# An LN, conv-gain and FFN block for 32,768 pixels on one core: group 4's last addition goes from an accumulating DMA to VectorE, and the rows of all engines are put in another order

## The chip, the cores and the metric

One of the eight cores of a Trainium2 chip. The metric is the device time of one execution in microseconds (us). The kernel is in Bass: each engine's instructions are written out in order, and engines meet only at semaphores.

## The reference

```python
def sobel_complexity(x): ...      # edge magnitude of the channel mean, per image
def adaptive_steps(m): ...        # a step of 1 to 5 for each pixel
def _forward(x):                  # "conv"
    V = v0 + v1 + v2 + v3         # how many of four walks visit a pixel
    return x * (V / (V + 1e-06))[:, None]

x = x + _forward(_ln_c(x))                         # x is (8, 24, 64, 64)
t = _to_tokens(x)                                  # 32768 tokens of 24 channels
y = q_acc(q_acc(q_mul(_ln_t(t)) @ q_mul(W1).T) + q_mul(b1))   # q_mul: 5 exponent, 2 mantissa bits
h = relu(y)                                                   # q_acc: 5 and 10 bits, 96 hidden
t = t + q_acc(q_acc(q_mul(h) @ q_mul(W2).T) + q_mul(b2))
```

After a layernorm over channels the channel mean is zero up to rounding, so the map of edges is flat and the walks take the same steps everywhere. The kernel has a flat pass with a constant share of visits, a flag that says if a channel mean was not zero, and a second pass behind a branch that runs only if it was. Here it does not run.

## The kernel before, in words

The pixels are in eight **groups** 0 to 7; a group is a tile of 128 partitions x 24 channels x 32 pixels in float32 (384 KB). The four statistics **units** are group 0, group 1, groups 2 and 3, and groups 4 to 7. For each group the work is this, with the helper's name and line:

- SP loads the pixels (L340). TensorE sums channels and squares (L579, L589, L607), ScalarE squares the centred pixels (`square`, L425).
- VectorE centres (`centre`, L806), sums the squares of a unit (`take_var`, L813), and works out the gain of a unit in three small instructions (`conv_gain`, L832 to L837). ScalarE takes roots (`first_std` L432, `second_std` L438), VectorE inverts them (`inverse_std` L820, `second_inverse` L849) and makes the second norm (`second_norm` L854).
- `conv` is result = centred x gain: on GpSimd (L372) for groups 0, 1, 2, 4, 5 and 6, on VectorE (L844) for 3 and 7. A wait on a count of VectorE's work ahead of `conv` on GpSimd sets its place.
- `quantise` (VectorE, L863) makes the fp8 input, TensorE turns it (`turn`, L625), ScalarE copies it (`copy_turned`, L447).
- The hidden layer has three parts: `first_layer` (TensorE, L640), `round_hidden` (ScalarE, L456), `bias_relu` (VectorE, L875) and `quantise_hidden` (VectorE, L884, in a piece of two parts and a piece of one).
- `second_layer` (TensorE, L662), `round_ffn` (ScalarE, L466), `second_bias` (VectorE, L892) give `ffn_out` in float16.
- The result is conv + pixels + ffn_out. The pixels are added by an accumulating DMA from GpSimd (`add_pixels`, L360). ffn_out is added by a second one (`add_ffn_by_dma`, L366) for groups 0 to 4, and by VectorE (`add_ffn`, L903) for 5 to 7. The semaphore residual[n] counts 16 for each landed DMA.
- SP stores the result (`store`, L327) in the order written out; the second half of group 7 is stored from ScalarE (`store_last`, L473).
- `unevenness` (VectorE, four instructions, L909 to L912), `find_peak` (TensorE, L616) and `flag` (VectorE, L919 and L920) make the flag. At its end each engine loads the flag (TENSOR_LOAD, L290) and takes a branch over the second pass (L769 TensorE, L1180 VectorE, L345 SP). `keep_busy` (L675) are TensorE matmuls whose result nobody reads.

The order on every engine is a list written out by hand in the functions `first_groups`. ScalarE reads four buffers of hidden rows; everything else has two.

## Time and profile before

| what | us |
|---|---|
| median of 3 runs | 67.58 |
| lowest and highest | 67.13 and 67.95 |
| the profiled execution's own time | 67.71 |
| its span, first to last instruction | 65.8 |
| VectorE busy | 54.9 (83%) |
| TensorE busy | 52.0 (79%) |
| ScalarE busy | 44.1 (67%) |
| GpSimd busy | 23.9 (36%) |

All times inside the execution are counted from the span's start. The 1.9 us between the span and the execution's own time lie outside it. VectorE is DVE in the rows, ScalarE ACT, GpSimd POOL, TensorE PE (its weight loads PEld), and a q behind a name is that engine's sequencer. Successive instructions of one engine overlap a little, so an instruction can take 0.48 us and the next one start 0.40 us behind its start.

### The profile page before, as it was taken

Reading aid. Unit: us, or ns where it says so; the run is one execution under the profiler, and the core shown is the slowest. Engines: PE = TensorE matmul, PEld = TensorE weight load, DVE = VectorE, ACT = ScalarE, POOL = GpSimd, SP = SyncE. Lnnn points to the kernel's source line nnn. Section 1 sums busy time; section 2 is a strip of 40 time slices with the busy share of each in tenths; the row PEclk is TensorE's granted clock in tenths of the full one; section 3 lists DMA queues with packets and bytes.
Section 4 is the critical chain, followed back from the end, with each engine's and each line's share of the span. In section 5 each row is a group of like instructions: output and inputs, shape, how many; then the busy total and the mean of one; then the engine's idle time right before and its main releaser. Section 6 shows DMA issues by size and latency. Waiting matters only on the chain.

```text
span 65.8 us, 1346 instructions
## 1 busy us (share of the span) xinstructions
PE 52.0 (79%) x471; PEld 36.5 (55%) x475; DVE 54.9 (83%) x113; ACT 44.1 (67%) x67; POOL 23.9 (36%) x25
## 2 busy tenths in 40 slices
PE   2999999999999999959759978979996988460000
PEld 0334999999998999826128335518262627150000
DVE  2059957899799999799999999999999999999300
ACT  5304352287749999279999999999999994450000
POOL 2000001964830000389387989962350580000000
PEclk9999999999999999999999999999999999999655
DMA  0999999009339000001995996999999399999651
GB/s 0 240 420 350 407 405 393 17 10 181 58 60 179 0 0 0 0 0 33 198 187 103 202 228 132 187 312 233 263 286 218 73 304 291 274 284 342 251 177 36
DMA packets 4475, 12.07 MB, mean 183 GB/s; under 512 B 496, under 2 KB 752, under 8 KB 4464
## 3 DMA queue, kind: packets, MB, share of 16 engines
q0 software_dynamic: 1872, 5.11, 39.1%
q1 hardware_dynamic: 2448, 6.62, 27.0%
q10 hardware_dynamic: 144, 0.20, 0.9%
q8 instruction: 6, 0.10, 0.8%
q14 instruction: 5, 0.04, 0.2%
HBM read 3.67 MB, written 3.15 MB: 104 GB/s over the span
## 4 chain that ended last, share of the span: by engine, by line
PE 49%; DVE 16%; ACT 13%; issue 12%; DVEq 2%; ACTq 0%
PE ps_ffn L607 12%; ACT hidden_rounded L456 10%; PE ps_ffn L589 8%; PE ps_ffn L764 8%; PE ps_hidden L640 6%; DVE hidden_q L884 5%; PE ps_ffn L662 5%; PE ps_ffn L579 4%; PE ps_hidden L607 4%; DVE ffn_out L892 3%; DVE hidden_act L875 2%; ACT packed_t L447 2%; DVE result L903 2%; DVE packed L863 1%; PE ps_turned L625 1%
## 5 line engine op out<-in xcount | busy, mean ns | idle before, releaser
L456 ACT ACTIVATE hidden_rounded<-ps_hidden 128x1024 f16<-128x1024 f32 x24 | 23.8, 1031 | 0.0
L372 POOL TENSOR_TENSOR result<-centred,gain 128x768 f32<-128x768 f32 x6 | 11.2, 1866 | 21.4 <-DVE scaled_var L837 10.4
L640 PE MATMUL ps_hidden<-packed_t,w1q 96*128 96x512 fp8e5 x48 | 14.0, 380 | 1.5 <-ACT packed_t L447 0.8
L875 DVE TENSOR_SCALAR hidden_act<-hidden_rounded,b1q 128x1024 f16<-128x1024 f16 x24 | 11.5, 478 | 0.0
L425 ACT ACTIVATE squares<-centred 128x768 f32<-128x768 f32 (+1 forms) x9 | 6.8, 769 | 4.6 <-DVE centred L806 4.6
L662 PEld LDWEIGHTS ps_ffn<-w2q,hidden_q 128*128 128x128 fp8e5 x168 | 7.6, 98 | 2.9 <-DVE hidden_q L884 2.4
L360 POOL DMA_DIRECT2D result<-loaded x8 | 8.4, 1103 | 1.8 <-POOL result L372 1.5
L662 PE MATMUL ps_ffn<-w2q,hidden_q 128*128 128x96 fp8e5 x168 | 8.3, 206 | 0.7 <-DVE hidden_q L884 0.7
L884 DVE TENSOR_SCALAR hidden_q<-hidden_act 128x2048 uint16<-128x2048 uint16 (+1 forms) x16 | 8.8, 549 | 0.1
L607 PEld LDWEIGHTS ps_ffn<-squares,loaded 128*128 128x128 f32 x72 | 8.6, 192 | 0.4
L607 PE MATMUL ps_ffn<-squares,loaded 128*128 128x128 f32 x72 | 8.7, 275 | 0.0
L806 DVE SCALAR_TENSOR_TENSOR centred<-ps_values,loaded 128x768 f32<-128x768 f32 (+1 forms) x9 | 7.5, 863 | 0.1
L863 DVE TENSOR_TENSOR packed<-centred,ps_values 128x768 fp8e5<-128x768 f32 x8 | 7.4, 946 | 0.0
L366 POOL DMA_DIRECT2D result<-ffn_out x5 | 4.6, 919 | 6.4 <-DVE ffn_out L892 5.9
L640 PEld LDWEIGHTS ps_hidden<-packed_t,w1q 96*128 96x128 fp8e5 x48 | 3.5, 98 | 5.4 <-ACT hidden_rounded L456 2.3
L466 ACT ACTIVATE ffn_rounded<-ps_ffn 128x768 f16<-128x768 f32 x7 | 5.7, 816 | 1.1 <-DVE ffn_out L892 1.0
L764 PE MATMUL ps_ffn<-warm 128*128 128x512 bf16 x12 | 5.3, 629 | 1.2 <-DVE warm L1175 1.2
L589 PE MATMUL ps_ffn<-loaded 128*128 128x128 f32 x48 | 5.7, 276 | 0.0
L589 PEld LDWEIGHTS ps_ffn<-loaded 128*128 128x128 f32 x48 | 5.5, 192 | 0.0
L786 DVE TENSOR_REDUCE ps_values<-loaded 128x32 f32<-128x768 f32 x2 | 3.0, 1482 | 2.8 <-DMA loaded<-in_load 2.8
L447 ACT ACTIVATE packed_t<-ps_turned 96x512 bf16<-96x512 bf16 x8 | 4.8, 599 | 0.5 <-PE ps_turned L625 0.4
L892 DVE TENSOR_TENSOR ffn_out<-ffn_rounded,b2q 128x768 f16<-128x768 f16 (+1 forms) x9 | 5.0, 562 | 0.0
(54 smaller groups left out, 54.5 us busy)
## 6 DMA issues: line engine op xcount, KB each, us to landing
result<-loaded POOLq DMA_DIRECT2D x8, 384.0 KB, 4.6
out<-result SPq DMA_DIRECT2D x7, 384.0 KB, 3.5
loaded<-in_load SPq DMA_DIRECT2D x6, 384.0 KB, 6.1
result<-ffn_out POOLq DMA_DIRECT2D x5, 384.0 KB, 5.2
loaded<-in_load SPq DMA_DIRECT2D x2, 448.0 KB, 4.1
loaded<-in_load SPq DMA_DIRECT2D x1, 385.5 KB, 7.8
out<-result SPq DMA_DIRECT2D x1, 192.0 KB, 2.5
out<-result ACTq DMA_DIRECT2D x1, 192.0 KB, 4.0
```

Of the source, the lines that this page charges most:

```text
L360: pool.dma_start(result[:, n], pixels[n], accum_op=ALU.add).then_inc(s.residual[n], 16)
L372: nc.gpsimd.tensor_tensor(result[:, n], centred[:, n], group_values(gain, n), ALU.mult).then_inc(s.conv_pool, 1)
L456: nc.scalar.activation(hidden_rounded[:, i % HIDDEN_BUFS], ps_hidden[:, i % 2], ACT.Copy).then_inc(s.hidden_rounded, 1)
L589: last = nc.tensor.matmul(ps_late_channels, ident, late_pixels[:, :, c, :], start=(c == 0), stop=(c == C - 1))
L607: last = nc.tensor.matmul(ps_square[u][:, n - UNIT_START[u]], ident, squares[:, n, c * GPIX:(c + CB) * GPIX], start=(c == 0), stop=(c == C ...
L640: last = nc.tensor.matmul(ps_hidden[:, i % 2, b * BANK:(b + 1) * BANK], w1q[:, t * P:(t + 1) * P], packed_t[:, n % 2].bitcast(E5M2)[:, b:: ...
L662: last = nc.tensor.matmul(ffn_banks(n)[:, half, at * CQ:(at + 1) * CQ], hidden_q[:, n % 2, t, col * P:(col + 1) * P].bitcast(E5M2)[:, 0::2 ...
L764: nc.tensor.matmul(ps_ffn[:, i % 2], warm[:, 0:P], warm[:], start=True, stop=True)
L806: nc.vector.scalar_tensor_tensor(centred[:, n, lo:hi, :], group_values(channel_sums, n)[:, lo:hi, :], -1.0 / C, pixels[n][:, lo:hi, :], AL ...
L863: nc.vector.tensor_tensor(packed[:, n % 2].rearrange("p j (c q) b -> p j c b q", q=Q), centred[:, n].rearrange("p c (j b q) -> p j c b q", ...
L875: nc.vector.tensor_scalar(hidden_act[:, n % 2, t], hidden_rounded[:, (n * TILES + t) % HIDDEN_BUFS], b1q[:, t:t + 1], 0.0, ALU.add, ALU.ma ...
L884: nc.vector.tensor_scalar(hidden_q[:, n % 2, lo:hi], hidden_act[:, n % 2, lo:hi].bitcast(U16), 1.0 / 256, None, ALU.mult).then_inc(s.hidde ...
```

## The change

Group 4's ffn_out is added by VectorE. One GpSimd DMA (L366) goes and one VectorE instruction (L903, 128x768 float32) comes. The lists of all five engines are rewritten: the list of SP stores group 2 behind groups 3 and 4; GpSimd issues the pixels of group 3 ahead of conv 2, has other counts to wait for ahead of convs 2, 4 and 5, and adds the pixels of group 7 one place earlier; VectorE's conv of group 7 and its four `unevenness` instructions are earlier. SP's branch over the second pass stands ahead of its wait for the stores, and the wait behind the branch. The number of instructions on TensorE, and of everything else but the one pair, stays.

```diff
-ADD_BY_DMA = range(0, 5)
-ADD_ON_VECTOR = range(5, NG)
+ADD_BY_DMA = range(0, 4)
+ADD_ON_VECTOR = range(4, NG)
...
                 store(s, 1)
-                store(s, 2)
                 store(s, 3)
                 store(s, 4)
+                store(s, 2)
                 store(s, 5)
...
-            sp.wait_ge(flat_pass.stored, 16 * (NG + 1))
             with sp.If(uneven_map):
+                sp.wait_ge(flat_pass.stored, 16 * (NG + 1))
...
                 sp.wait_ge(uneven_pass.stored, 16 * (NG + 1))
+            sp.wait_ge(flat_pass.stored, 16 * (NG + 1))
...
                 add_pixels(s, 1)
-                pool.wait_ge(s.hidden_act, 4)
+                add_pixels(s, 3)
+                pool.wait_ge(s.hidden_q, 2)
                 conv(s, 2)
                 add_pixels(s, 2)
-                add_pixels(s, 3)
-                pool.wait_ge(s.hidden_act, 6)
+                pool.wait_ge(s.hidden_act, 5)
                 conv(s, 4)
+                add_ffn_by_dma(s, 0)
                 add_pixels(s, 4)
-                add_ffn_by_dma(s, 0)
-                pool.wait_ge(s.hidden_act, 9)
+                pool.wait_ge(s.hidden_act, 7)
                 conv(s, 5)
...
                 add_ffn_by_dma(s, 3)
-                add_ffn_by_dma(s, 4)
                 add_pixels(s, 7)
```

TensorE, in the middle of the statistics. Before, the matmuls of the squares of groups 4 and 5 and those of groups 6 and 7 (L607) are parted by a first layer (L640; the trace counts each float32 matmul twice):

```order
L607 MATMUL ps_ffn<-squares,loaded 128x128 x12
L640 MATMUL ps_hidden<-packed_t,w1q 128x512 x2
L607 MATMUL ps_ffn<-squares,loaded 128x128 x12
L640 MATMUL ps_hidden<-packed_t,w1q 128x512 x4
L625 MATMUL ps_turned<-ident_bf,packed 96x128 x4
L662 MATMUL ps_ffn<-w2q,hidden_q 128x96 x24
```

After:

```order
L607 MATMUL ps_ffn<-squares,loaded 128x128 x24
L640 MATMUL ps_hidden<-packed_t,w1q 128x512 x4
L662 MATMUL ps_ffn<-w2q,hidden_q 128x96 x24
L640 MATMUL ps_hidden<-packed_t,w1q 128x512 x2
L625 MATMUL ps_turned<-ident_bf,packed 96x128 x4
```

The last statistics come one first layer earlier, and the second layer of group 0 comes ahead of a first layer and a turn.

VectorE, from the last statistics (`take_var(3)`, L813) on. Before:

```order
L875 TENSOR_SCALAR hidden_act<-hidden_rounded,b1q 128x1024
L813 TENSOR_REDUCE square_sums<-ps_ffn 128x128
L863 TENSOR_TENSOR packed<-centred,ps_values 128x96x2x4
L820 RECIPROCAL inv_std<-std 128x128
L875 TENSOR_SCALAR hidden_act<-hidden_rounded,b1q 128x1024
L832 TENSOR_TENSOR gain<-loaded,inv_std 128x128
```

After:

```order
L884 TENSOR_SCALAR hidden_q<-hidden_act 128x1024
L813 TENSOR_REDUCE square_sums<-ps_ffn 128x128
L863 TENSOR_TENSOR packed<-centred,ps_values 128x96x2x4
L820 RECIPROCAL inv_std<-std 128x128
L875 TENSOR_SCALAR hidden_act<-hidden_rounded,b1q 128x1024
L832 TENSOR_TENSOR gain<-loaded,inv_std 128x128
```

One `bias_relu` (L875) that stood ahead of the last statistics now stands behind them.

VectorE, near the end, with the flag (L919, L920) and the additions (L903). Before:

```order
L919 TENSOR_REDUCE peak<-ps_turned 1x1
L920 TENSOR_SCALAR uneven<-peak 1x1
L875 TENSOR_SCALAR hidden_act<-hidden_rounded,b1q 128x1024
L892 TENSOR_TENSOR ffn_out<-ffn_rounded,b2q 128x8x24x4
L884 TENSOR_SCALAR hidden_q<-hidden_act 128x2048
L875 TENSOR_SCALAR hidden_act<-hidden_rounded,b1q 128x1024
L884 TENSOR_SCALAR hidden_q<-hidden_act 128x1024
L903 TENSOR_TENSOR result<-result,ffn_out 128x768
```

After:

```order
L903 TENSOR_TENSOR result<-result,ffn_out 128x768
L884 TENSOR_SCALAR hidden_q<-hidden_act 128x1024
L875 TENSOR_SCALAR hidden_act<-hidden_rounded,b1q 128x1024
L919 TENSOR_REDUCE peak<-ps_turned 1x1
L920 TENSOR_SCALAR uneven<-peak 1x1
L884 TENSOR_SCALAR hidden_q<-hidden_act 128x2048
L875 TENSOR_SCALAR hidden_act<-hidden_rounded,b1q 128x1024
L892 TENSOR_TENSOR ffn_out<-ffn_rounded,b2q 128x8x24x4
L884 TENSOR_SCALAR hidden_q<-hidden_act 128x1024
L903 TENSOR_TENSOR result<-result,ffn_out 128x768
```

The first L903 is group 4's, ahead of the last pieces of group 6. Behind the last L884 nothing changes.

## Rows read from the trace of the kernel before

**Rows 1.** The page, part 1, and the rows DVE and DMA of part 2.

```profile
PE 52.0 (79%) x471; PEld 36.5 (55%) x475; DVE 54.9 (83%) x113; ACT 44.1 (67%) x67; POOL 23.9 (36%) x25
...
DVE  2059957899799999799999999999999999999300
...
DMA  0999999009339000001995996999999399999651
```

**Rows 2.** Busy time by stretch: us, then each engine's, PEclk, DMA share, GB/s.

```profile
28.00:38.00 10.00, 7.74 (x80) 4.09 (x79) 9.93 (x20) 9.52 (x14) 7.92 (x7) 1.00 0.66 120
38.00:48.00 10.00, 8.79 (x87) 4.62 (x87) 10.00 (x21) 10.00 (x15) 6.38 (x6) 1.00 0.97 232
48.00:57.30 9.30, 7.48 (x90) 4.27 (x89) 9.13 (x22) 7.66 (x9) 3.10 (x3) 1.00 0.90 238
57.30:61.50 4.20, 1.19 (x24) 1.05 (x24) 3.95 (x8) 0.98 (x2) 0.00 (x0) 0.98 0.99 311
```

**Rows 3.** Timeline of VectorE: start, us, instruction, idle ahead and who ended it.

```profile
26.80 0.49 DVE L875 TENSOR_SCALAR hidden_act<-hidden_rounded,b1q 128x1024 f16<-128x1024 f16 x1
27.72 0.69 DVE L813 TENSOR_REDUCE square_sums<-ps_ffn 128x128 f32<-128x512 f32 x1 [0.44 <-PE ps_ffn L607]
...
37.97 1.04 DVE L892 TENSOR_TENSOR ffn_out<-ffn_rounded,b2q 128x768 f16<-128x768 f16 x1
38.93 0.68 DVE L884 TENSOR_SCALAR hidden_q<-hidden_act 128x2048 uint16<-128x2048 uint16 x1
...
44.61 0.55 DVE L892 TENSOR_TENSOR ffn_out<-ffn_rounded,b2q 128x768 f16<-128x768 f16 x1
45.08 0.48 DVE L875 TENSOR_SCALAR hidden_act<-hidden_rounded,b1q 128x1024 f16<-128x1024 f16 x1
...
57.30 0.95 DVE L903 TENSOR_TENSOR result<-result,ffn_out 128x768 f32<-128x768 f32 x1
58.17 0.55 DVE L892 TENSOR_TENSOR ffn_out<-ffn_rounded,b2q 128x768 f16<-128x768 f16 x1
...
60.43 1.03 DVE L903 TENSOR_TENSOR result<-result,ffn_out 128x384 f32<-128x384 f32 x2
```

**Rows 4.** Timeline of TensorE at the last squares.

```profile
24.41 0.60 PE L640 MATMUL ps_hidden<-packed_t,w1q 96*128 96x512 fp8e5 x2
24.84 2.84 PE L607 MATMUL ps_ffn<-squares,loaded 128*128 128x128 f32 x24
```

**Rows 5.** Timeline of ScalarE around its last wait for statistics.

```profile
25.68 1.02 ACT L456 ACTIVATE hidden_rounded<-ps_hidden 128x1024 f16<-128x1024 f32 x1
28.45 0.40 ACT L432 ACTIVATE std<-square_sums,eps_c 128x128 f32<-128x128 f32 x1 [1.76 <-DVE square_sums L813]
28.76 1.00 ACT L456 ACTIVATE hidden_rounded<-ps_hidden 128x1024 f16<-128x1024 f32 x1
```

**Rows 6.** Timeline of GpSimd at convs 4 and 5.

```profile
32.43 1.80 POOL L372 TENSOR_TENSOR result<-centred,gain 128x768 f32<-128x768 f32 x1 [1.01 <-DVE hidden_act L875]
34.53 0.88 POOL L360 DMA_DIRECT2D result<-loaded  x1 [0.30 <-POOL result L372]
...
36.46 2.13 POOL L372 TENSOR_TENSOR result<-centred,gain 128x768 f32<-128x768 f32 x1
```

**Rows 7.** Last sequencer instructions: branches of TensorE, VectorE and SP, drains (L151), with durations in ns.

```profile
L769 PEldq COMPARE_BRANCH  x1: 5297/5297/5297, 58.9 to 58.9; - x1
...
L1180 DVEq COMPARE_BRANCH  x1: 72/72/72, 61.5 to 61.5; - x1
...
L345 SPq COMPARE_BRANCH  x1: 45/45/45, 65.5 to 65.5; - x1
...
L151 DVEq DRAIN  x1: 62/62/62, 64.8 to 64.8; - x1
L151 SPq DRAIN  x1: 7/7/7, 65.6 to 65.6; - x1
```

**Rows 8.** DMA queue q0 (GpSimd's), and issues: KB each, median us to landing.

```profile
q0 software_dynamic: 1872, 5.11, 39.1%
...
out<-result SPq DMA_DIRECT2D x1, 192.0 KB, 2.5
out<-result ACTq DMA_DIRECT2D x1, 192.0 KB, 4.0
```

**Rows 9.** DMA queue q8 (code) in 60 to 62 us: packets, MB, share of 16 engines.

```profile
q8 instruction: 1, 0.02, 6.1%
```

**Rows 10.** DMA busy share in 40 slices of the stretch 62.8 to 65.3 us.

```profile
DMA  9899894331132041121211111111111100900000
```

More of the change, by code:

```diff
@@ L721, in first_groups @@
                 second_layer(s, 0)
+                first_layer(s, 1, 2)
+                turn(s, 2)
                 first_layer(s, 2, 0)
                 first_layer(s, 2, 1)
+                turn(s, 3)
                 keep_busy(s, 1)
-                turn(s, 3)
                 first_layer(s, 2, 2)
@@ L1101, in first_groups @@
                 inverse_std(2)
+                conv_gain(s, 2)
                 bias_relu(s, 0, 0)
-                conv_gain(s, 2)
+                conv(s, 3)
                 bias_relu(s, 0, 1)
-                conv(s, 3)
+                quantise_hidden(s, 0, 0, 2)
                 second_inverse(s, 2)
-                quantise_hidden(s, 0, 0, 2)
                 bias_relu(s, 0, 2)
+                second_norm(s, 2)
                 quantise_hidden(s, 0, 2, 3)
-                second_norm(s, 2)
-                bias_relu(s, 1, 0)
                 take_var(3)
@@ L1114, in first_groups @@
                 inverse_std(3)
+                bias_relu(s, 1, 0)
+                conv_gain(s, 3)
+                second_bias(s, 0)
                 bias_relu(s, 1, 1)
-                conv_gain(s, 3)
-                quantise_hidden(s, 1, 0, 2)
-                bias_relu(s, 1, 2)
                 quantise(s, 3)
                 second_inverse(s, 3)
+                bias_relu(s, 1, 2)
+                quantise_hidden(s, 1, 0, 2)
+                second_norm(s, 3)
+                quantise_hidden(s, 1, 2, 3)
                 bias_relu(s, 2, 0)
-                quantise_hidden(s, 1, 2, 3)
-                second_bias(s, 0)
-                bias_relu(s, 2, 1)
-                second_norm(s, 3)
-                bias_relu(s, 2, 2)
                 quantise(s, 4)
                 quantise(s, 5)
+                bias_relu(s, 2, 1)
                 second_bias(s, 1)
+                bias_relu(s, 2, 2)
                 quantise_hidden(s, 2, 0, 2)
@@ L1141, in first_groups @@
                 second_bias(s, 2)
+                conv(s, 7)
                 bias_relu(s, 4, 2)
@@ L1147, in first_groups @@
                 second_bias(s, 3)
+                bias_relu(s, 5, 2)
                 quantise_hidden(s, 5, 0, 2)
-                bias_relu(s, 5, 2)
-                conv(s, 7)
                 bias_relu(s, 6, 0)
+                unevenness()
+                bias_relu(s, 6, 1)
                 quantise_hidden(s, 5, 2, 3)
-                bias_relu(s, 6, 1)
+                bias_relu(s, 6, 2)
                 second_bias(s, 4)
-                unevenness()
-                bias_relu(s, 6, 2)
+                bias_relu(s, 7, 0)
                 quantise_hidden(s, 6, 0, 2)
-                bias_relu(s, 7, 0)
+                add_ffn(s, 4)
                 quantise_hidden(s, 6, 2, 3)
+                bias_relu(s, 7, 1)
                 flag()
-                bias_relu(s, 7, 1)
-                second_bias(s, 5)
                 quantise_hidden(s, 7, 0, 2)
                 bias_relu(s, 7, 2)
+                second_bias(s, 5)
                 quantise_hidden(s, 7, 2, 3)
```

22 lines of the change are left out of this document (10 added, 12 removed).

## The prediction

> **What bounds the kernel now.** I read the page first. VectorE is the busiest engine with 54.9 us, and the digits of its row are 9s from about 28 us to 61 us [rows 1]. The stretches say it in us: 9.93 of 10.00, 10.00 of 10.00, 9.13 of 9.30 (a gap of 0.1 us here and there), 3.95 of 4.20 [rows 2]. ScalarE is as full from 38 to 48 us, but has air behind it. So until 61.5 us VectorE's list of instructions is the clock, and whatever lengthens that list counts in full unless a wait goes.
>
> Then I looked for what VectorE still loses. The timeline has one real wait in that part, 0.44 us ahead of the last statistics at 27.72 us, for TensorE's squares. It also has one instruction of odd length: the second_bias of group 1 at 37.97 us took 1.04 us where its like at 44.61 us took 0.55 [rows 3]. It came while GpSimd ran conv 5 (36.46 for 2.13 us, to 38.59) [rows 6]. VectorE's last addition ends at 60.43 + 1.03 = 61.46 us.
>
> Behind it come 4.4 us without any computing. Two chains run there, and this is the part that the eye misses. The first: the last store is issued from ScalarE at 61.5 and lands 4.0 us later, at 65.5, though an equal one of SP needs 2.5 [rows 8]. SP's branch is at 65.5, its drain at 65.6 [rows 7], and a barrier ends the span at 65.8. The DMA row shows why 4.0: from about 63.6 to 64.9 us the share is one tenth, so one or two of sixteen DMA engines still have packets and the rest are through [rows 10]. The second: VectorE's branch is at 61.5 and its drain only at 64.8, 3.3 us later; TensorE's branch, which jumps as far, is shown with 5.30 us [rows 7]. So with the store gone, the execution would still end at about 64.8 + 0.2 = 65.0 us (65.04 with the digits of the trace). The tail has a floor of 3.6 us behind VectorE's last addition, and the store hangs 0.8 us over it.
>
> The Trainium skill has a rule for the second chain (Runtime: NRT & Kernel Launch, "Instruction fetch mechanics"): a taken branch whose target is outside the two pages at hand has to fetch the target page by DMA before the engine can go on. The 5.30 us and 3.3 us agree with it.
>
> **The change part by part.** All of it against this execution: span 65.8 us, time 67.71.
>
> *The addition of group 4.* One float32 L903 of 128x768. In the list such an instruction takes 58.17 - 57.30 = 0.87 us up to the next start [rows 3]. VectorE has no air between 28 and 57.3 us to hide it [rows 2]: **+0.87 us**. Its data are there: the pixels of group 4 are added by a DMA issued at 34.53 us [rows 6], 20 us ahead.
>
> *The last statistics.* TensorE now does the squares of groups 6 and 7 right behind 4 and 5. The first layer between them took 24.84 - 24.41 = 0.43 us [rows 4], so take_var(3) can start at 27.29 instead of 27.72. The inputs are there: ScalarE squares groups 6 and 7 back to back and does the root and the copy behind. **-0.43 us**. But one bias_relu that was ahead of take_var now stands behind it. That kind has a duration of 0.48 us [rows 3] and overlaps the next by about 0.08 (second_bias at 44.61 took 0.55 and the next started 0.47 behind it): **+0.40 us**. The two nearly cancel. The wait of 0.44 us itself stays nearly as long: its end is 0.43 us nearer, and the work ahead of it is 0.40 us shorter.
>
> *ScalarE.* It waited 1.76 us there and restarted at 28.45 with first_std(3); it had done the rounding at 25.68 (group 1's first part) before [rows 5]. Now that rounding comes behind, so ScalarE restarts 0.43 earlier with 0.91 us more to do: it runs 0.3 to 0.5 us late from then on. Who waits? second_bias(0), which moves up to directly behind conv_gain(3). By my walk VectorE gets there at 30.85 us and the rounded ffn at 31.0: **+0.15 us**. second_inverse(3) follows by a margin near zero. Further on the consumers run 1 us and more behind ScalarE, and where they had come closest (second_bias(4)) the list now has the four unevenness instructions ahead; I charge nothing.
>
> *GpSimd against VectorE.* The conv on GpSimd seems to hold something that a half-precision VectorE instruction needs: that is my reading of 1.04 for 0.55 us [rows 3, 6]. Conv 5 now starts behind the first bias_relu of group 2 instead of the third, and VectorE's two quantise instructions of groups 4 and 5 follow there (0.86 us each from start to start), so conv 5 should be done when second_bias(1) comes: **-0.49 us**. Against it: conv 5 (1.8 us at the least) outlasts two quantises (1.72), and the gate opens about when GpSimd gets free from two DMA issues of 0.88 us. The bias_relu behind the quantises may wait up to 0.35 us, and one behind conv 4 about 0.13. Between 0.0 and +0.5 for the two; I take **+0.20**.
>
> The Trainium skill says of it (SBUF — State Buffer, "Who interferes with whom"): VectorE and GpSimd share one pair of ports as an exclusive lock, and the second to issue blocks fully. The long second_bias ends within 0.5 us of conv 5's end, which agrees. The rule also speaks against this change, since it names a tensor_tensor with both inputs in SBUF, the form of the new L903; but no conv of GpSimd is left near 54 us, so the sum is the same with it.
>
> Sum on VectorE: 0.87 - 0.43 + 0.40 + 0.15 - 0.49 + 0.20 = **+0.70 us**, with ends 0.3 (no collision at all) and 1.2 (the gain of 0.49 doesn't come). Its end goes from 61.46 to about 62.15.
>
> *The removed DMA.* q0 carried 13 accumulates and took 39.1% of 16 engines' 65.8 us: 25.7 / 13 = 1.98 us of all sixteen engines each [rows 8]. That is work of 2 us off a resource that is 90 to 99% busy from 38 to 61.5 us [rows 2]. But nothing on an engine waits for it before the tail. The pixels of group 7 are issued behind group 3's ffn and no longer behind group 4's, so the accumulates end some 3 us sooner. The stores run as late as VectorE lets them: group 4's right behind its addition at about 54.9, group 2's behind that (its result lay ready, the queue of SP is what it waits for), then 5, 6 and 7. Two stores at 55 us have 3 us until group 5's, enough.
>
> *The tail.* The floor moves with VectorE: 65.04 + 0.70 = 65.74. The last store starts at 62.2. If it still needs 4.0 us the end is 65.8 + 0.70 - 0.1 = 66.4; if it needs the 2.5 us of its like [rows 8] it is done at 64.7 and the floor rules. Between them I choose near the floor. I take the straggling DMA engines to be late because of code: one packet of q8 held one of the sixteen for 6.1% of 16 x 2 us, 1.95 us, between 60 and 62 us [rows 9], and what lay behind it on that engine were the packets of four stores. In the changed kernel fewer packets lie there, since the accumulates and the stores of groups 4 and 2 are through; it takes 0.65 us of catching up to reach the floor, and 1.5 are to be had. SP's branch before its last wait takes 65.6 - 65.5, some 0.1 us, off the store's chain and nothing off the floor. Its code is now loaded near 62 us, beside the last stores: at worst 0.4 us on one DMA engine.
>
> Sum: the likeliest span is 65.75 to 65.85, no more than 0.1 from today's 65.8. Outside the span 1.9 as before. The profiled execution stood 0.13 over the median of 67.58, so the **forecast is 67.5 us**: no change that three runs can show. (I call within 1%, 0.68 us, the same; the three runs of before spread over 0.82 us.)
>
> **The rivals.**
>
> *The tail shortens for real (faster).* VectorE's code load is a DMA too, and it starts among the stores. If lighter queues bring the 3.3 us from branch to drain down by 0.7, and VectorE's list grows by the lower end of 0.3 only, then 65.04 + 0.3 - 0.7 = 64.6, so 1.2 us less: 66.4 us. For it: the share of 0.99 up to 61.5 us [rows 2] and TensorE's 5.30 against VectorE's 3.3. Against it: at VectorE's branch the load had only the last stores beside it, as it will have now.
>
> *Convs of GpSimd meet half-precision instructions (slower).* If the new gates of convs 4 and 5 leave them a step late, each falls on a bias_relu or second_bias for the 0.49 us of [rows 3]; with the saved 0.49 not saved that is 0.87 - 0.43 + 0.40 + 0.15 + 2 x 0.49 = 1.97 on VectorE, 65.04 + 1.97 = 67.0, so +1.2: 68.8 us. It decides from the point where both convs start more than one bias_relu (0.4 us) behind their gates. For it: GpSimd has two issues ahead of conv 5, and here conv 5 started at once behind one of them, not behind its gate [rows 6].
>
> *The store doesn't catch up (a little slower).* 4.0 us again behind a VectorE that ends 0.70 later: 66.4, so 68.1 with 0.1 off for the median. It counts as the same by 1%.
>
> *The change of adder does nothing, the order alone does.* The DMA work that goes was hidden; then only 0.87 is paid and the result is that of my sum. This is contained in the forecast.
>
> **How the numbers follow.** Forecast with its ends 67.1 to 68.1: 0.56, the third rival's 0.12 of these. Shorter tail: 0.26. Collisions: 0.18. Range: from 66.6 (most of the first rival) to 68.3 (part of the second): 0.8. Faster than 66.9: 0.26; within 1%: 0.56; slower than 68.26: 0.18.
>
> **What would show it.** In the profile of the changed kernel: take_var(3) at 27.3 us; second_bias of group 1 at 0.55 us and not 1.04; VectorE's last addition ending between 61.8 and 62.6, with no idle over 0.2 us from 28 us on; no L366 for group 4, and q0 through by 56 us; the last store landing in less than 3.4 us, and VectorE's drain 3.3 us behind its branch as the last thing but the barrier. The prediction is wrong if VectorE waits for ScalarE more than once between 30 and 50 us, if its list ends by 61.5, or if the distance from branch to drain isn't fixed.

## The result, and the profile after

The changed kernel took **68.96 us** (median of 4 runs, 68.12 to 69.55) and the kernel before 67.39 us in the same job (4 runs, 67.13 to 67.95): ratio 1.017, interval 1.009 to 1.025. It was forecast at 67.5 us, no difference; it is slower. The changed kernel was timed again in three later jobs, beside the kernel before on the same chip. The table pools all its runs, and for before those of all six later jobs. The ratios, here and below, leave disturbed runs out; medians and the table keep them.

| | runs | fastest | lowest tenth | lowest quarter | median | median span |
|---|---|---|---|---|---|---|
| before | 104 | 66.67 | 66.96 | 67.27 | 67.72 | 65.9 |
| changed | 28 | 67.30 | 67.57 | 68.10 | 68.78 | 66.85 |
| difference | | +0.63 | +0.61 | +0.83 | +1.06 | +0.95 |

The bootstrap interval of the median's difference is 0.66 to 1.41 us, that of the lowest tenth's 0.32 to 1.14. With before's runs from the changed kernel's own four jobs alone (57 runs, median 67.61) the difference is 1.17 us (0.75 to 1.56). So there are two questions: where 0.6 us come from that every execution pays, and why the middle of the runs lies 0.4 further up.

The profiled execution of the changed kernel took 68.70 us, 0.99 over the one of before (67.71). Its page, parts 1 to 3 and 6, the rows that answer to [rows 1] and [rows 8]:

```profile
PE 51.3 (77%) x471; PEld 36.1 (55%) x475; DVE 55.6 (84%) x114; ACT 43.9 (66%) x67; POOL 22.6 (34%) x24
...
DVE  2069946899799999898999999999999999999600
...
DMA  0899999108519000842904999979993995926561
...
q0 software_dynamic: 1728, 4.72, 36.5%
...
out<-result SPq DMA_DIRECT2D x1, 192.0 KB, 2.6
out<-result ACTq DMA_DIRECT2D x1, 192.0 KB, 3.4
```

VectorE has one instruction more and 0.7 us more to do, q0 has 144 packets less. Now the stretches that answer to [rows 2]; the last one is longer by the us that VectorE ends later:

```profile
28.00:38.00 10.00, 7.71 (x80) 4.32 (x80) 9.82 (x19) 9.59 (x14) 7.79 (x6) 1.00 0.54 107
38.00:48.00 10.00, 8.73 (x84) 4.49 (x82) 10.00 (x21) 10.00 (x14) 5.74 (x6) 1.00 0.98 229
48.00:57.30 9.30, 8.00 (x90) 4.45 (x93) 9.16 (x23) 7.63 (x11) 1.81 (x2) 1.00 0.81 210
57.30:62.50 5.20, 1.59 (x26) 1.05 (x24) 4.96 (x10) 1.64 (x3) 0.00 (x0) 0.96 0.56 215
```

VectorE is as full as before, and the DMA share is lower where the accumulate went (0.81 for 0.90; from 57.3 to 61.5 us alone 0.49 for 0.99), which nobody on VectorE had waited for. Its timeline, the places of [rows 3]:

```profile
9.80 0.29 DVE L813 TENSOR_REDUCE square_sums<-ps_hidden 128x32 f32<-128x128 f32 x1 [0.97 <-PE ps_hidden L607]
...
27.68 0.69 DVE L813 TENSOR_REDUCE square_sums<-ps_ffn 128x128 f32<-128x512 f32 x1 [0.22 <-PE ps_ffn L607]
...
31.04 0.29 DVE L837 SCALAR_TENSOR_TENSOR scaled_var<-gain,scaled_once 128x128 f32<-128x128 f32 x1
31.44 0.56 DVE L892 TENSOR_TENSOR ffn_out<-ffn_rounded,b2q 128x768 f16<-128x768 f16 x1
...
38.30 0.55 DVE L892 TENSOR_TENSOR ffn_out<-ffn_rounded,b2q 128x768 f16<-128x768 f16 x1
...
54.52 0.95 DVE L903 TENSOR_TENSOR result<-result,ffn_out 128x768 f32<-128x768 f32 x1
55.38 0.42 DVE L884 TENSOR_SCALAR hidden_q<-hidden_act 128x1024 uint16<-128x1024 uint16 x1
...
61.44 1.03 DVE L903 TENSOR_TENSOR result<-result,ffn_out 128x384 f32<-128x384 f32 x2
```

The first statistics start at 9.80 us. Before it was 9.41: the third load landed 0.61 us later, and that is no work of the change. The new addition at 54.52 holds VectorE for 0.86 us. The second_bias of group 1, 1.04 us before, takes 0.55. The last addition ends at 62.47 us, 1.01 later, so the list itself (from the first statistics to the end) went from 52.05 to 52.66 us, +0.61.

The last sequencer instructions, which answer to [rows 7]:

```profile
L769 PEldq COMPARE_BRANCH  x1: 4357/4357/4357, 59.3 to 59.3; - x1
...
L1181 DVEq COMPARE_BRANCH  x1: 72/72/72, 62.5 to 62.5; - x1
...
L343 SPq COMPARE_BRANCH  x1: 50/50/50, 63.3 to 63.3; - x1
...
L151 DVEq DRAIN  x1: 63/63/63, 65.4 to 65.4; - x1
L151 SPq COMPARE_BRANCH  x1: 38/38/38, 65.9 to 65.9; - x1
L151 SPq DRAIN  x1: 7/7/7, 66.1 to 66.1; - x1
```

VectorE's drain comes 2.9 us behind its branch (before 3.3), TensorE's branch is shown with 4.36 us (5.30), and SP, whose branch over the second pass is now at 63.3 and its wait for the stores behind it, leaves that wait at 65.9: the last store is still what ends last, 0.5 us behind VectorE's drain. It landed 3.4 us after its issue (before 4.0), just where the prediction had put its sign ("less than 3.4 us"); the last accumulate had landed at 55.2 us, before the 56 that it asked for. The 0.99 us of the two profiled executions are then 0.39 (head) + 0.61 (VectorE's list) - 0.57 (tail: from 4.38 to 3.81 us) + 0.56 (outside the span: from 1.86 to 2.42 us).

### The profile page after: what moved, and what is told of

Its sections match the earlier page's. It is cut to its first block and busy times, and to the rows that moved or that the text cites. A ratio compares the mean times of both kernels' runs of the same rounds, so it can differ in the third digit from the quotient of the medians.

```text
span 66.3 us, 1347 instructions
## 1 busy us (share of the span) xinstructions
PE 51.3 (77%) x471; PEld 36.1 (55%) x475; DVE 55.6 (84%) x114; ACT 43.9 (66%) x67; POOL 22.6 (34%) x24
## 5 line engine op out<-in xcount | busy, mean ns | idle before, releaser
L640 PE MATMUL ps_hidden<-packed_t,w1q 96*128 96x512 fp8e5 x48 | 14.1, 381 | 3.6 <-ACT packed_t L447 2.4
L875 DVE TENSOR_SCALAR hidden_act<-hidden_rounded,b1q 128x1024 f16<-128x1024 f16 x24 | 11.7, 487 | 0.0
L884 DVE TENSOR_SCALAR hidden_q<-hidden_act 128x2048 uint16<-128x2048 uint16 (+1 forms) x16 | 8.8, 551 | 0.0
L607 PEld LDWEIGHTS ps_ffn<-squares,loaded 128*128 128x128 f32 x72 | 8.4, 192 | 0.3
L607 PE MATMUL ps_ffn<-squares,loaded 128*128 128x128 f32 x72 | 8.5, 275 | 0.0
L640 PEld LDWEIGHTS ps_hidden<-packed_t,w1q 96*128 96x128 fp8e5 x48 | 3.4, 97 | 8.4 <-ACT packed_t L447 3.5
L367 POOL DMA_DIRECT2D result<-ffn_out x4 | 3.8, 955 | 4.4 <-DVE ffn_out L892 4.3
L764 PE MATMUL ps_ffn<-warm 128*128 128x512 bf16 x12 | 4.1, 516 | 1.2 <-DVE warm L1176 1.2
L675 PE MATMUL ps_ffn<-warm 128*128 128x512 bf16 x15 | 4.2, 380 | 0.8 <-ACT ffn_rounded L466 0.7
```

Source lines behind the costliest of these rows:

```text
L607: last = nc.tensor.matmul(ps_square[u][:, n - UNIT_START[u]], ident, squares[:, n, c * GPIX:(c + CB) * GPIX], start=(c == 0), stop=(c == C ...
L640: last = nc.tensor.matmul(ps_hidden[:, i % 2, b * BANK:(b + 1) * BANK], w1q[:, t * P:(t + 1) * P], packed_t[:, n % 2].bitcast(E5M2)[:, b:: ...
L875: nc.vector.tensor_scalar(hidden_act[:, n % 2, t], hidden_rounded[:, (n * TILES + t) % HIDDEN_BUFS], b1q[:, t:t + 1], 0.0, ALU.add, ALU.ma ...
L884: nc.vector.tensor_scalar(hidden_q[:, n % 2, lo:hi], hidden_act[:, n % 2, lo:hi].bitcast(U16), 1.0 / 256, None, ALU.mult).then_inc(s.hidde ...
```

## The experiments

"Stretch" is the time from VectorE's first statistics (the first L813) to the end of its last addition in the profiled execution; it leaves out the scatter of the loads. "Tail" is from there to the span's end.

**The changed kernel again**, without an edit, three times.

> The changed kernel once more, against the kernel before on the same chip. First theory (several parts): VectorE's list is 0.6 us longer, the time outside the span is 0.5 us longer (2.4 against 1.9 in the two profiled executions), and 0.4 us was only a late load: ratio 1.010 to 1.020, with the squares of the first unit at 9.4 us again. Rival (chance): both the late load and the 0.5 us outside are scatter of single executions: ratio 1.003 to 1.010.

> The changed kernel a third time, to tell a cost from scatter. First theory now: VectorE's list is 0.64 us longer, the tail 0.6 to 0.8 shorter, so the undisturbed spans are 65.4 to 65.8 against 65.1 to 65.6 of before (+0.2 to +0.4 us); and in about a third of the executions the time outside the span is 2.2 to 2.4 us and not 1.8 to 1.9 (it was in 5 of 16 so far, and in none of 37 with group 4 added by a DMA). Rival: both are scatter, and the fast runs stand within 0.1 us of before.

> The changed kernel once more, to have enough executions for the middle and the lower quartile. From the profiles so far: from the first take_var to VectorE's end 52.65 us against 52.05 of before, whatever the load did; tail 3.3 to 3.8 us against 3.7 to 4.4. So quiet executions +0.3 to +0.6 us over before, and the median +0.3 to +1.2.

Measured: medians 68.26 (12 runs), 68.98 (6) and 68.58 us (6), ratios 1.003 (0.998 to 1.009), 1.026 (1.021 to 1.031) and 1.018 (1.011 to 1.026); stretches 52.65, 53.37 and 53.25 us, tails 3.60, 3.73 and 3.66. Intervals of single jobs that don't meet are a warning: a verdict on this kernel wants pooled runs and, above all, stretches. The stretches of again2 and again3 are told below; their clock fell.

**SP's branch.** Before, with the branch ahead of the wait for the stores; and the changed kernel with SP's old order.

```diff
 # e1_sp_branch, on before; e3_old_branch takes the same off the changed kernel
-            sp.wait_ge(flat_pass.stored, 16 * (NG + 1))
             with sp.If(uneven_map):
...
+            sp.wait_ge(flat_pass.stored, 16 * (NG + 1))
```

> The kernel before with one edit: SP takes its branch over the second pass before it waits for the stores. First theory: this edit is what puts 0.5 us outside the span (a load of SP's code that comes after the last instruction): time +0.4 to +0.6 us, with the span the same or 0.1 shorter. Rival: the place of the branch costs nothing: time within 0.2 us of before. My prediction had -0.1 us at the store's chain.

> The changed kernel with SP's branch put back behind the wait for the stores. First theory: 0.4 to 0.6 us faster than the changed kernel, so +0.5 to +0.8 us over the kernel before, and the time outside the span 1.9 us. Rival (the branch is free): as the changed kernel, +0.9 to +1.4 us.

Measured: 67.47 us, 0.998 (0.993 to 1.003, 12 runs); and 68.63 us, 1.016 (1.007 to 1.026, 6 runs), stretch 52.65. SP's branch is not what costs.

**The adder alone, and the addition alone.** In before: group 4 added by VectorE, all else as it was; then one spare VectorE addition at the same place, with the DMA kept.

```diff
 # e2_adder_only
-ADD_BY_DMA = range(0, 5)
-ADD_ON_VECTOR = range(5, NG)
+ADD_BY_DMA = range(0, 4)
+ADD_ON_VECTOR = range(4, NG)
...
-                add_ffn_by_dma(s, 4)
...
+                add_ffn(s, 4)
 # e5_spare_add
+                nc.vector.tensor_tensor(spare[:], centred[:, 4], ffn_out[:, 4], ALU.add)
```

> The kernel before with one edit: group 4's ffn is added by VectorE (behind the first hidden part of group 7) and its accumulating DMA is gone; all other orders and SP's branch as before. First theory: +0.87 us on VectorE, less what the tail gives back (0 to 0.8 us, since the last store hung 0.8 us over the floor): +0.1 to +0.9 us. Rival (the reordering is what costs): within 0.1 us of before.

> The kernel before with one more VectorE instruction of the form and at the place of group 4's addition, which writes a tile that nobody reads; group 4 is still added by its DMA. First theory: +0.87 us on VectorE, and the tail gives nothing back: +0.8 to +1.0 us. If the last store catches up behind a later VectorE: +0.3 to +0.8. Time outside the span 1.8 to 1.9 us if it is GpSimd's program that matters.

Measured: 69.25 us, 1.013 (1.002 to 1.024, 8 runs); 69.64 us, 1.028 (1.020 to 1.037, 6 runs). The stretches are 52.90 and 52.91, against 52.05 of before: +0.85 and +0.86, the forecast's 0.87. e2_adder_only's ratio comes to 0.9 us, which is its list. The rest of the 1.9 us by which e5_spare_add stands over that job's 67.70 isn't in its list: its profile shows the first statistics at 10.61, behind a late load, and a tail of only 3.34.

**The DMA alone.** Before without the second accumulate of group 4; nobody adds that group's ffn, so this part of the output is left out.

```diff
-                eng.wait_ge(s.residual[n], 32)
+                eng.wait_ge(s.residual[n], 16 if n == 4 and s is flat_pass else 32)
...
-                add_ffn_by_dma(s, 4)
```

> The kernel before with group 4's second accumulating DMA left out and nothing in its place (group 4's result lacks its ffn): what the removed DMA alone was worth. First theory: VectorE ends at the same time, the last store hung 0.8 us over the floor of VectorE's code load, so -0.1 to -0.8 us, likeliest -0.3, and the time outside the span stays 1.8 to 1.9 us, since VectorE's program is as before. Rival (the DMA was hidden altogether): within 0.1 us. If the longer time outside the span comes from GpSimd's shorter program, it shows here: 2.2 to 2.4 us in a third of the runs.

Measured: 67.84 us, 1.007 (1.002 to 1.011, 13 runs), stretch 52.04. The forecast had been -0.1 to -0.8 us. Taking 2 us of work off all DMA engines gains nothing: it was hidden.

**The orders alone.** The changed kernel with group 4 added by the DMA again; run in two jobs.

```diff
-ADD_BY_DMA = range(0, 4)
-ADD_ON_VECTOR = range(4, NG)
+ADD_BY_DMA = range(0, 5)
+ADD_ON_VECTOR = range(5, NG)
```

(and store 4, the DMA and the addition put back to match).

> The changed kernel with group 4 added by its DMA again (SP stores group 2 before 4): the new orders alone. First theory: VectorE's list ends 0.2 us sooner than before (0.64 less 0.87), and the store of the tail binds as before or a little less: -0.2 to -0.6 us against before, and 1.8 to 1.9 us outside the span. Rival (the new order costs by itself): +0.2 us or more.

> The new orders with group 4 still added by its DMA, again: in its one profile VectorE needed 51.78 us from the first take_var to its end, 0.27 less than before. If only that counts: fastest runs 0.1 to 0.3 us below the fastest of before, median within 0.4. If the adder alone makes the loss of the changed kernel, this median stands 0.6 us or more below it.

Measured: 68.36 and 68.69 us, 1.015 (1.007 to 1.022) and 1.013 (1.004 to 1.023), 6 runs each; stretches 51.78 and 51.81 us, so the orders shorten VectorE's list by 0.27 and 0.24 us. VectorE's last addition in e6_order_only, 0.44 us sooner than in [rows 3]:

```profile
9.24 0.29 DVE L814 TENSOR_REDUCE square_sums<-ps_hidden 128x32 f32<-128x128 f32 x1 [0.28 <-PE ps_hidden L608]
...
59.99 1.03 DVE L904 TENSOR_TENSOR result<-result,ffn_out 128x384 f32<-128x384 f32 x2
```

Adder and orders add up: 0.86 - 0.26 = +0.60, and the changed kernel with a whole clock shows 52.65 or 52.66 (after, again, e3_old_branch, e15_filled_wait). But the runs don't get faster by the 0.27: the fastest, 67.14 us, is no better than before's, and the middle is worse. By the ratios the orders alone lose 0.9 to 1.0 us and the adder alone 0.9, so the times of the two don't add up as their lists do. The orders bring something with them that the list doesn't show.

**Where the branch lands.** Instructions that never run, in the second pass, move the code that the branch jumps to: 32 in the changed kernel, 2 in before.

```diff
+                if h == 0:
+                    for _ in range(32):      # 2 in e8_moved_landing
+                        step(nc.vector.memset(pad_a[:], 0.0))
```

> The changed kernel with 32 more VectorE instructions and their waits inside the second pass, which is jumped over and never runs: VectorE's landing place behind its branch lies 64 places further on. The time outside the span was 2.2 to 2.4 us in 12 of 36 executions of the kernels with one more VectorE instruction ahead of the branch, and in none of 73 others. If the landing place makes that (where it stands in a page of code), none of these runs shows it: 1.8 to 1.9 us in all, and the median falls by about 0.1 to 0.2 us. If the instructions executed ahead of the branch make it: still 2.2 to 2.4 us in about a third of the runs.

> The kernel before with two more VectorE instructions and their waits inside the second pass that never runs: the landing place moves by 4, as in the changed kernel, and nothing executed changes. If the landing place makes the longer time outside the span: 2.2 to 2.4 us in about a third of the runs. If not: 1.8 to 1.9 us in all. The spans as before in either case.

Measured: 67.85 us, 1.013 (1.003 to 1.022, 6 runs), tail 3.31; 67.75 us, 1.002 (0.997 to 1.008, 12 runs), tail 3.68. The time outside the span was 2.2 to 2.4 us in two of e7_padded_branch's six runs and never in e8_moved_landing's twelve, so the landing place isn't what makes it. In e8_moved_landing VectorE's drain, 3.40 us behind the branch, came last, and this is before's own list: the tail of 4.38 us on which the prediction was made is not what before always has.

**First half old, warm-up, number of instructions.** The changed kernel with the first-half lists of before on all engines; with 16 warm matmuls at its start for 12; with two clears moved from VectorE to GpSimd; and before with two tiny clears more.

```diff
 # e9_front_old, of many lines
-                pool.wait_ge(s.hidden_act, 5)
+                pool.wait_ge(s.hidden_act, 6)
...
 # e10_warm16
-WARM = 12
+WARM = 16
 # e11_fewer_vector
-            nc.vector.memset(table_warm[:], 1.0)
-            link(nc.vector.memset(quad[:], 0.0))
+            nc.gpsimd.memset(table_warm[:], 1.0).then_inc(eps_ready, 1)
+            nc.gpsimd.memset(quad[:], 0.0).then_inc(eps_ready, 1)
 # e12b_more_vector, on before
+            nc.vector.memset(table_spare[:, 0:1], 1.0)
+            nc.vector.memset(table_spare[:, 1:2], 1.0)
```

> The changed kernel with the orders of the first half (up to the hidden part of group 2 on VectorE) as before, the second half and the adder as changed. Theory: the new first half saves VectorE 0.2 us in a quiet execution but leaves TensorE waiting 1.3 us at 30.6 us, behind which the granted clock sometimes falls (in one profile from 33.3 to 36.7 us), and that is why the middle run of the changed kernel is 1 us over its quiet ones. Then this kernel's quiet spans are 0.2 longer (65.6 to 66.0), but its median span is below the changed kernel's (66.4 to 67.1). Rival (the adder makes it): median span no better than the changed kernel's.

> The changed kernel with 16 matmuls ahead of the first load and not 12: cover for a late third load. In two profiles of slow executions the third load landed at 7.5 to 7.8 us and the granted clock was then at half for 3.4 us. Theory: fewer executions with spans over 67.5 us, quiet ones the same or up to 0.2 us longer. Rival: the late load costs as much by itself, and as many runs are slow.

> The changed kernel with two small clears at the start (table_warm and quad) moved from VectorE to GpSimd: VectorE executes 112 instructions and not 114, nothing else moves. So far the time outside the span was over 2.1 us in 19 of 60 executions of the kernels with one more executed VectorE instruction (114) and in 0 of 102 of those with 113. If the number of executed VectorE instructions makes that: 1.8 to 1.9 us in all runs, and the mean time 0.15 us below the changed kernel's. If the work at the end of VectorE's list makes it: over 2.1 us in a third.

> The kernel before with two more one-column clears on VectorE at its start, to two different columns; they delay nothing. Executions with over 2.1 us outside the span have come only in kernels whose executed VectorE list differs from the one of before (23 of 101), also with the same number of instructions (the orders alone: 3 of 12). If a changed list alone makes it: over 2.1 us in a fifth to a third of the runs. If the time at which VectorE ends beside the others makes it: 1.8 to 1.9 us in all, spans as before.

Measured: 68.28 us, 1.013 (1.003 to 1.023), stretch 52.84; 68.59 us, 1.013 (1.004 to 1.023), stretch 52.64; 68.88 us, 1.016 (1.007 to 1.026), stretch 54.05 (its clock fell); 67.82 us, 1.006 (1.001 to 1.012, 12 runs, the others 6), stretch 52.35. Four more warm matmuls (two of e10_warm16's six spans are still 67.5 us and more) or fewer clears cure nothing. With the old first half the stretch is 0.19 us longer, so most of what the orders gain lies there; its median span of 66.45 us and its fastest of 65.9 came out as its theory asked, but with six runs, a ratio no better and a median span of 66.2 of before in the same job, that shows little. In e12b_more_vector the two clears, which were to delay nothing, stand beside a stretch 0.30 us longer: nearly all of it is at one bias_relu at 30.23 us that starts 0.24 us late and runs longer. One stretch, too, can be a draw.

**Before against itself**, as if it were a changed kernel, to see what a job can pretend.

> The kernel before, unchanged, run as if it were a changed one, against itself: what the comparison shows of nothing. If the scatter of a build (where code and tensors lie in memory) makes part of what I ascribe to the change: a median up to 1 us over the other runs of before, or executions with over 2.1 us outside the span. If not: ratio within 0.995 to 1.005, all 1.8 to 1.9 us outside the span.

Measured: 68.14 us against 67.97, 1.003 (0.997 to 1.008, 13 runs). Its profiled execution took 70.21 us (span 68.3), and the reason lies in the head. By stretch (us, each engine's busy time, PEclk, DMA share, GB/s):

```profile
6.00:8.00 2.00, 0.00 (x0) 0.00 (x0) 2.00 (x3) 0.94 (x2) 0.00 (x0) 0.96 0.87 340
8.00:10.00 2.00, 1.82 (x8) 1.86 (x9) 1.05 (x2) 0.84 (x1) 0.00 (x0) 0.50 1.02 404
10.00:12.00 2.00, 2.00 (x15) 2.00 (x14) 0.00 (x0) 0.00 (x0) 0.00 (x0) 0.68 0.95 380
```

and TensorE there:

```profile
8.18 2.90 PE L579 MATMUL ps_ffn<-loaded 128*128 128x128 f32 x12 [2.62 <-DMA loaded<-in_load]
```

The third load landed at 8.04 us, TensorE had nothing for 2.62 us, and the granted clock fell to half (1.2 of 2.4 GHz) for 3.4 us. The first statistics came at 12.60 instead of 9.41 us. It happened in three of the twenty profiles (e2_adder_only and e4_no_ffn4 as well, all three with before's orders), so it doesn't need the change; it is a reason why the upper half of the runs says little. A late load isn't enough for it: in e5_spare_add the third load landed at 7.52 us, but the warm matmuls lasted until 6.53 us (here until 5.56), TensorE waited only 1.13 us, and the clock stayed up.

**TensorE's wait filled.** This answers what again2 and again3 showed. The new first-half order lets TensorE turn group 2 and then wait for ScalarE, whose copy of it comes behind `round_ffn` of group 0. In again2, ScalarE's timeline, then TensorE's:

```profile
30.71 0.81 ACT L466 ACTIVATE ffn_rounded<-ps_ffn 128x768 f16<-128x768 f32 x1
31.40 0.59 ACT L447 ACTIVATE packed_t<-ps_turned 96x512 bf16<-96x512 bf16 x1
```

```profile
30.40 0.39 PE L625 MATMUL ps_turned<-ident_bf,packed 128*96 128x128 bf16 x4
32.05 0.60 PE L640 MATMUL ps_hidden<-packed_t,w1q 96*128 96x512 fp8e5 x2 [1.26 <-ACT packed_t L447]
32.95 0.89 PE L640 MATMUL ps_hidden<-packed_t,w1q 96*128 96x512 fp8e5 x2 [0.30 <-ACT hidden_rounded L456]
33.63 0.63 PE L625 MATMUL ps_turned<-ident_bf,packed 128*96 128x128 bf16 x4
34.06 1.49 PE L675 MATMUL ps_ffn<-warm 128*128 128x512 bf16 x3
```

and its stretches:

```profile
31.00:33.00 2.00, 0.65 (x3) 0.16 (x4) 1.85 (x5) 2.00 (x4) 0.33 (x1) 1.00 0.93 173
33.00:35.00 2.00, 2.00 (x9) 1.02 (x10) 2.00 (x4) 2.00 (x4) 2.00 (x2) 0.54 0.20 36
35.00:37.00 2.00, 2.00 (x11) 0.81 (x10) 2.00 (x5) 1.05 (x3) 2.00 (x3) 0.61 0.53 126
37.00:39.00 2.00, 2.00 (x31) 1.29 (x28) 1.55 (x3) 2.00 (x4) 1.70 (x2) 1.00 1.04 203
```

TensorE works 0.65 of 2 us from 31 to 33 us, and behind it the granted clock stands at half for 3.4 us; the first layers take 0.8 to 0.9 us a pair for 0.6, ScalarE waits (1.05 busy of 2.00) and then VectorE (1.55 of 2.00). The kernel before, and the changed kernel in its first profile, in the same stretch:

```profile
31.00:33.00 2.00, 1.41 (x5) 0.33 (x5) 1.97 (x5) 2.00 (x4) 0.99 (x2) 1.00 1.08 198
```

```profile
31.00:33.00 2.00, 0.83 (x3) 0.23 (x4) 1.86 (x5) 2.00 (x5) 0.52 (x1) 1.00 1.05 195
33.00:35.00 2.00, 1.76 (x10) 0.65 (x9) 2.00 (x4) 2.00 (x4) 2.00 (x2) 1.00 0.08 14
```

Before works 1.41 us there. The hole isn't always followed by a fall. It is 1.26 us in all ten profiles with the new first half (this edit's aside), and three of them have the fall (again2, again3, e11_fewer_vector: stretches 0.7, 0.6 and 1.4 us longer); of the nine with the old first half none. The mean granted clock, on record for every run, points the same way: it was below 0.96 in 31 of 64 runs of the programs with the new first half (this edit's again aside) and in 50 of 186 of those with the old one. Below 0.95 the two hardly differ (9 of 64 and 18 of 186), and the figure doesn't say where in a run the clock fell. The edit, in the changed kernel:

```diff
+                pe.wait_ge(s.hidden_rounded, 5)
+                for _ in range(4):
+                    nc.tensor.matmul(ps_hidden[:, 0, 0:BANK], warm[:, 0:P], warm[:], start=True, stop=True)
                 first_layer(s, 2, 0)
```

> The changed kernel with one thing added: ahead of the first layer of group 2 (second half) TensorE waits for the count that group 1's hidden tile gives, and then runs 4 warm matmuls into a bank that the next layer overwrites, so that its 1.26 us wait there (30.6 to 31.9 us) is filled with matmuls. Nothing is left out. Theory A: the emptied stretch lets the granted clock fall to 0.5 for 3.4 us at 33 to 37 us in some executions (three of the ten profiles with this order in the first half, none of nine without it), and that holds the middle of the changed kernel's runs up. Then the clock of 28 to 60 us stays at 1.00, VectorE's stretch from its first take_var to its end is 52.6 to 52.8 us, the median span is 66.3 or less (66.85 pooled for the changed kernel) and the fastest span stays at 65.4 to 65.8, since quiet executions have nothing to gain. Rival B: the middle of the runs is held up by something else (the head's loads, the time outside the span): the median span stays at 66.5 to 67.2 and the ratio at 1.013 to 1.02. Rival C: the added matmuls come late and delay the first layer behind them: VectorE's stretch grows by up to 0.4 us, to 53.0.

Measured: 68.24 us, 1.014 (1.007 to 1.020, 6 runs). The wait is gone, the clock whole, the stretch 52.65 us. TensorE's timeline, then stretches:

```profile
30.81 1.04 PE L724 MATMUL ps_hidden<-warm 128*128 128x512 bf16 x4
31.99 0.60 PE L640 MATMUL ps_hidden<-packed_t,w1q 96*128 96x512 fp8e5 x2
```

```profile
31.00:33.00 2.00, 1.56 (x7) 0.41 (x6) 1.86 (x5) 2.00 (x4) 0.39 (x1) 1.00 0.95 175
33.00:35.00 2.00, 1.94 (x11) 0.67 (x10) 2.00 (x4) 2.00 (x4) 2.00 (x2) 1.00 0.18 34
```

The median span is 66.35 us, against 66.85 pooled of the changed kernel, where theory A asked for 66.3 or less. But before's median span in this job was 65.6, so a difference of 0.75 us is still there (pooled it was 0.95), the fastest span is 66.1 and not 65.4 to 65.8, and the ratio lies where rival B wanted it. Rival C falls: the list isn't longer. One profile with a whole clock proves little where seven of ten have it anyway. So that the fall hangs on the wait is not settled; that the fall, once there, costs 0.6 to 1.4 us, is shown by the stretches. Its tail was 4.30 us, the last store landing 3.9 us after its issue, in a kernel without the accumulate.

## Why the prediction was wrong

**The list of VectorE: right.** The forecast of +0.70 (0.3 to 1.2) measured +0.60. Of the terms, the adder's 0.87 measured 0.85 and 0.86 (e2_adder_only, e5_spare_add). The others were to sum to -0.17 and measured -0.26 (e6_order_only, e13_order_again). The take_var that was to come 0.43 us sooner did (17.88 us behind the first statistics, before 18.31), and the bias_relu behind it cost 0.39. The -0.49 of the second_bias of group 1 came, 1.04 to 0.55 us. The last statistics were to start at 27.3 us and did so: 27.68 less the 0.39 of the head is 27.29.

second_bias(0) was charged 0.15 for a wait, and it came: it started 0.40 us behind the instruction at 31.04, where before's next instruction there started 0.21 behind, and ScalarE had ended the rounding it needs at 31.33; that is 0.19. The collisions of convs 4 and 5 were charged 0.20. The bias_relu wholly inside conv 4 took 0.54 us (at 34.03), but one inside conv 4 took 0.54 in before too (at 33.98), so that is no cost of the change; the one at 37.80, at the end of conv 5, took 0.58 for 0.48, so the collisions cost about 0.10. Another 0.10 is at 46.14 us (0.58), where GpSimd runs no conv, and 0.12 came back at the last bias_relu. Before, VectorE:

```profile
31.05 0.29 DVE L837 SCALAR_TENSOR_TENSOR scaled_var<-gain,scaled_once 128x128 f32<-128x128 f32 x1
31.26 0.69 DVE L884 TENSOR_SCALAR hidden_q<-hidden_act 128x2048 uint16<-128x2048 uint16 x1
...
33.98 0.54 DVE L875 TENSOR_SCALAR hidden_act<-hidden_rounded,b1q 128x1024 f16<-128x1024 f16 x1
```

After, ScalarE and then VectorE:

```profile
30.52 0.81 ACT L466 ACTIVATE ffn_rounded<-ps_ffn 128x768 f16<-128x768 f32 x1
...
34.03 0.54 DVE L875 TENSOR_SCALAR hidden_act<-hidden_rounded,b1q 128x1024 f16<-128x1024 f16 x1
...
37.80 0.58 DVE L875 TENSOR_SCALAR hidden_act<-hidden_rounded,b1q 128x1024 f16<-128x1024 f16 x1
```

The Trainium skill's rule on the shared port pair (SBUF — State Buffer, "Who interferes with whom") agrees with the 0.49 us that came back once conv 5 no longer lay beside that instruction. This is one row before and one after; no experiment moved the conv alone. The bias_relus inside a conv, at 0.54 us, weren't blocked.

**The wait for ScalarE: right.** The view of waits has only one of VectorE from 28 to 50 us, the 0.22 us for TensorE ahead of the last statistics; none is for ScalarE; the one in front of second_bias(0) is a gap of 0.11 us, too short for that view. The prediction didn't look at TensorE there, though. ScalarE's list, which it walked only to see whether VectorE would wait, is also what TensorE waits for: its copy of group 2 comes behind round_ffn(0), and a hole of 1.26 us opens.

**The failed step: the tail.** The step was "the store hangs 0.8 us over" the floor, so VectorE's +0.70 would be paid out of it and "no more than 0.1" would be left. It read one execution's tail of 4.38 us as before's tail. Eight profiles with the accumulate kept show 4.38, 4.19, 3.34, 4.22, 4.65, 3.68, 4.23 and 3.68 us, in the mean 4.05; twelve without it 3.81, 3.60, 3.73, 3.66, 4.30, 3.56, 3.68, 3.31, 3.29, 3.39, 3.65 and 4.30, in the mean 3.69. The tail gives back 0.36 us in the mean (bootstrap interval 0.02 to 0.68) and not 0.6 to 0.7. The two first profiles would have hidden this: there it gave back 0.57 of VectorE's 0.61. The lowest tenth of the runs is +0.61 us, as if the quickest executions got nothing back; that the store is at the floor in them in either kernel would explain it, but no profile caught such a pair, and its interval is wide. e4_no_ffn4 is the nearest test: the accumulate taken away and no addition put in its place should have gained up to 0.8 by this step, and gained nothing. So even the 0.36 can't be put down to the accumulate.

That the last store is late because of a code packet was only argued. The packet of q8 that the prediction named can't be it in every case: in e15_filled_wait its like ran from 60.44 to 61.65 us, the last store was issued a us later, at 62.61, and still took 3.9 us, in a kernel without the accumulate. A later packet of q8 (63.98 us, 1.24 us long) lies inside that store; whether it held it up is open.

The floor itself wasn't fixed either, which the prediction had named as a way to be wrong: from VectorE's branch to its drain it took 2.90 to 3.01 us in six profiles, 3.1 to 3.4 in eleven, 3.77 in both runs of the orders alone and 3.82 in e2_adder_only. One and the same program can repeat it (3.77 and 3.77) or not (2.90, 3.31, 3.38 and 3.29 of the changed kernel). The Trainium skill (Runtime: NRT & Kernel Launch, "Instruction fetch mechanics") has the taken branch fetch its target page by DMA. If the stores slowed that fetch, its time would vary as it does here, but no run separated the two.

**Two terms put at nothing: the middle of the runs.** The fall of the clock is not in the prediction. Three in ten times 0.9 us is +0.27 in the mean, an estimate from three profiles. The time outside the span, "1.9 as before", was 2.2 to 2.4 us in 6 of 28 runs of the changed kernel (in three of its first four) and in none of 104 of before: +0.10. With VectorE's +0.60 and the tail's -0.36 that makes +0.61 in the mean; measured is +0.87 (0.46 to 1.29). The 0.26 between them is inside the interval and has no cause shown.

**Open.** What makes the longer time outside the span: it isn't SP's branch (e3_old_branch has it in 3 of 6 runs), nor the orders (e2_adder_only and e5_spare_add have it), nor the addition (e13_order_again has it in 3 of 6, e6_order_only, the same program, in none), nor the landing place (e7_padded_branch has it in 2 of 6), nor the number of VectorE's instructions by itself (e12b_more_vector with two more has it in none of 12, e13_order_again with before's number in 3). e11_fewer_vector has it in none of 6, which is too few to say that fewer cure it. In the profile of after a last code packet starts 2.1 us behind the span's end; the queue's row for 66 to 70 us:

```profile
q14 instruction: 1, 0.01, 0.9%
```

It is there at 68.4 us in after and as far behind the end in e7_padded_branch and e10_warm16, the other two profiled executions with over 2.1 us outside the span; in the others no packet starts later than 0.4 us behind the end. Open too is why e5_spare_add, which lengthens VectorE's list by 0.86 without new orders, came out 1.9 us slower, and why the orders alone, whose list is 0.26 shorter, have a median span of 66.55 us in both jobs (before 65.9 and 65.7). Their two tails, 4.22 and 4.65 us, are among the longest. No version tried was faster than the kernel before.

**The rivals.** The shorter tail didn't come: lighter queues didn't speed up VectorE's way out by 0.7, though 0.4 was seen in single profiles. GpSimd's convs met half-precision instructions for about 0.1 us, not twice 0.49, and the price itself was wrong for one kind: a bias_relu wholly inside a conv took 0.54 us for 0.48, so the 0.49 holds for second_bias alone. The median ended near that rival's 68.8 by another way. "The store doesn't catch up" (68.1) was nearest in mechanism, though its chance was counted inside the forecast.

## What to carry to other kernels

An instruction added to a list without air costs its whole start-to-start time, and taking away the DMA that it replaces gains nothing unless somebody waits for it. A slack read from one profile, above all a tail between two chains, is one draw of a scatter: take several profiles before spending it on a cost. And where an order is rewritten for the busiest engine, look at the holes that it opens on TensorE, since a hole can be followed by microseconds at half clock.

## What the runs showed of the hardware

- From its taken branch over the second pass to its drain VectorE needed 2.9 to 3.8 us (twenty profiles), and TensorE's branch was shown with 3.5 to 5.3 us.
- TensorE idle for 2.62 us in the head was followed by 3.4 us at a granted clock of half; idle for 1.26 us in mid-kernel, by the same in three of ten profiles.
- A float16 tensor_tensor of 128x768 took 1.04 us beside GpSimd's conv and 0.55 without it; a float16 tensor_scalar of 128x1024 wholly inside a conv took 0.54 us for 0.48.
- Equal stores of 192 KB landed in 2.2 to 2.8 us from SP's queue and in 2.9 to 4.2 us from ScalarE's, issued half a us later.
- A kernel measured against itself in one job gave 1.003 with an interval of 0.997 to 1.008, but the same changed kernel gave 1.017, 1.003, 1.026 and 1.018 in four jobs.
